# First batch of a relative-attention layer: keys of all chunks projected first, ones written by ScalarE, loads placed singly

## The reference

```python
rk, rv = embK[dist], embV[dist]
logits = einsum('bhqd,bhkd->bhqk', q, k) + einsum('bhqd,qkd->bhqk', q, rk)
w = softmax(logits)
out = einsum('bhqk,bhkd->bhqd', w, v) + einsum('bhqk,qkd->bhqd', w, rv)
out = out.reshape(tokens, 256) @ Wo.T + bo
```

## Time and profile before

| | us |
|---|---|
| median of 3 runs | 2489.82 |
| profiled execution, its time | 2489.01 |
| its span, first to last instruction | 2487.2 |
| TensorE busy in the span | 2360.2 (95%) |
| VectorE busy | 2072.3 (83%) |
| ScalarE busy | 1533.3 (62%) |
| GpSimd busy | 955.0 (38%) |

### The profile page before, as it was taken

One profiled execution on the slowest core, in us unless ns is written; L12 is line 12 of the kernel. 1 busy time (PEld: TensorE's weight loads), 2 busy tenths in 40 slices (PEclk: granted clock), 3 DMA queues, 4 the chain that ended last, 5 costly groups with the idle time before them and its releaser, 6 DMA issues.

```text
span 2487.2 us, 100503 instructions
## 1 busy us (share of the span) xinstructions
PE 2360.2 (95%) x41858; PEld 1743.2 (70%) x41858; DVE 2072.3 (83%) x5306; ACT 1533.3 (62%) x2993; POOL 955.0 (38%) x2219
## 2 busy tenths in 40 slices
PE   4599999999999999999999999999999999999995
PEld 3277777777777777777777777777777777777773
DVE  5588789987898878987899878998789887998886
ACT  2366666666666666666666666666666666666651
POOL 5001634435343444425444263443534344442024
PEclk8699999999999999999999999999999999999998
DMA  4766675567656576565755667466765657656520
GB/s 137 230 194 181 201 206 149 163 176 220 182 155 184 166 209 191 158 182 180 200 171 166 189 194 205 147 169 179 216 187 149 183 174 206 194 144 192 153 57 30
DMA packets 659031, 433.24 MB, mean 174 GB/s; under 512 B 204304, under 2 KB 657680, under 8 KB 658448
## 3 DMA queue, kind: packets, MB, share of 16 engines
q1 hardware_dynamic: 655632, 424.52, 58.7%
q10 hardware_dynamic: 2944, 2.29, 0.3%
HBM read 231.30 MB, written 194.79 MB: 171 GB/s over the span
## 4 chain that ended last, share of the span: by engine, by line
PE 67%; DVE 23%; issue 6%; SPq 2%; ACT 1%; POOL 1%; DMA 1%; DVEq 0%; POOLq 0%; ACTq 0%
PE logitsT L955 16%; PE oacc L979 14%; PE scores L928 10%; DVE junk L1231 7%; PE logitsT L959 7%; DVE maxes L1225 7%; PE misc L883 5%; PE misc L1004 2%; PE misc L991 2%; PE misc L1043 2%; PE misc L900 2%; PE misc L911 2%; DVE stats L1101 2%; PE misc L1015 1%; DVE mv L1104 1%
## 5 line engine op out<-in xcount | busy, mean ns | idle before, releaser
L955 PE MATMUL logitsT<-qs,ks 98*128 98x128 bf16 (+1 forms) x8192 | 878.4, 221 | 7.6 <-ACT wy L1445 3.0
L1231 DVE CUSTOM_DVE_ANT_1 junk<-scores,bands 128x512 bf16<-128x512 f32 x988 | 679.6, 688 | 188.5 <-issue 79.1
L1445 ACT ACTIVATE wy<-logitsT 128x512 f32<-128x512 f32 x1024 | 561.6, 596 | 375.0 <-PE logitsT L955 367.7
L1225 DVE TENSOR_REDUCE maxes<-scores 128x1 f32<-128x512 f32 x1024 | 656.6, 682 | 81.8 <-PE scores L928 79.2
L955 PEld LDWEIGHTS logitsT<-qs,ks 98*128 98x128 bf16 (+1 forms) x8192 | 582.9, 99 | 183.5 <-issue 96.4
L928 PE MATMUL scores<-mks,mqs 48*128 48x256 bf16 (+6 forms) x3712 | 445.0, 289 | 20.5 <-DMA mks<-kd 10.8
L959 PE MATMUL logitsT<-ident,bands 128*128 128x128 f32 x2048 | 410.3, 278 | 0.9 <-issue 0.9
L1445 ACT ACTIVATE wr<-logitsT 128x512 f32<-128x512 f32 x512 | 314.3, 614 | 127.8 <-PE logitsT L955 126.3
L1474 POOL TENSOR_SCALAR rs<-rs 128x1 int32<-128x1 int32 (+1 forms) x217 | 46.4, 214 | 716.5 <-DVE rs L1106 709.5
L959 PEld LDWEIGHTS logitsT<-ident,bands 128*128 128x128 f32 x2048 | 292.7, 143 | 20.4
L1479 POOL TENSOR_SCALAR rs<-rs 128x1 f32<-128x1 f32 x744 | 279.2, 378 | 64.9
(11 more groups left out here) (145 smaller groups left out, 2951.9 us busy)
## 6 DMA issues: line engine op xcount, KB each, us to landing
bs<-praw SPq DMA_DIRECT2D x256, 512.0 KB, 4.5
bands<-bs SPq DMA_DIRECT2D x224, 512.0 KB, 4.5
ks<-kd SPq DMA_DIRECT2D x64, 384.0 KB, 5.0
qs<-qd SPq DMA_DIRECT2D x112, 198.0 KB
bands<-bs SPq DMA_DIRECT2D x128, 128.0 KB, 2.8
mks<-kd SPq DMA_DIRECT2D x128, 96.0 KB, 3.7
qd<-qparts SPq DMA_DIRECT2D x60, 192.0 KB, 3.5
qd<-qparts SPq DMA_DIRECT2D x90, 128.0 KB, 3.1
```

What stands on the lines that cost most here:

```text
L955: mm = e.matmul(lt[:, j * P:(j + 1) * P], kk[0:depth, SLOT[HB * blk + j], kt * P:(kt + 1) * P], qs[i][0:depth, SLOT[HB * blk + j], :], sta ...
L1225: e.tensor_reduce(top, sc[:], AX.X, ALU.max).then_inc(row_maxed, 1)
L1231: e.tensor_tensor_reduce(junk[:], sc[:].rearrange("p (a c) -> p a c", a=2), banded, 1.0, LOWEST, ALU.add, ALU.max, top).then_inc(row_maxed, 1)
L1445: e.activation(dst, src, ACT.Exp).then_inc(exp_ready, 1)
```

## The change

It concerns the first batch and the order of what stands before the body:

- Every stage of every chunk of the first batch has a slot of its own, and so has every load, band product, band write and band read of steps 0 to 3. The order on TensorE becomes: turn chunk 0, its queries and keys, far; turn 1, keys 1; turn 2, keys 2; turn 3, keys 3; queries 1, band products of step 0, queries 2, the values of all four chunks, queries 3, band products. SP's list begins: write queries 0, tables, write far 0 and keys 0, load of the queries of step 0, write keys 1, loads of keys 0, write keys 2, and so on; the loads of `mqs` for step 0 stand behind the band reads of step 0.
- The turned tokens of the first batch go to four buffers in `wm` (`xnT0`), the whole values to two (`qf` and `qf1`, in `wy`), and the two buffers of parts alternate by turn of each kind.
- The ones of `ks` and `mks` are copied by ScalarE from one column (`set_ones`, four stages), not set by GpSimd.
- The root of the variance of chunk 1 is taken on VectorE, as that of chunk 0 was.
- `ternary` moves from slot 17.5 to 70.7, three tables are loaded early, two later.
- Weights wait for the keys of their chunk, and every exp of kind Y for the queries and keys of all four chunks to be in DRAM.
- A table `MOVED` of offsets is added; all are zero.

```diff
-    return k == (0, 0) if stage == "statistics" else last_tile(*k) and k[1] % 2 == 1
+    return k in ((0, 0), (0, 1)) if stage == "statistics" else last_tile(*k) and k[1] % 2 == 1
...
- 'write_reltab': -60,
- 'load_table': (-20.0, 3.085, 5.0, 7.0, 9.0),
- 'ternary': 17.535,
+ 'write_reltab': 7.195,
+ 'load_table': (-87.418, -93.996, -1.974, -89.271, 15.194),
+ 'ternary': 70.73,
...
- 'first_chunk': (-100.964, -90.0, -76.951, -69.582),
- 'first_statistics': (-108.7, -102.706, -101.999, -102.4),
- 'first_normalise': (-102.964, -96.591, -89.5, -79.5),
- 'first_stages': (-0.488, 0.47, 2.57, 4.15, 4.77, 5.8, 6.17, 6.12),
- 'keys_first_stages': (-2.295, 4.08, 6.368, 1.463, 3.0, 8.5, 8.999, 5.33),
- 'first_load_k': (-83.694, -73.717, -63.8, -62.01),
- 'first_load_q': (-89.075, -77.2, -63.496, -53.6),
- 'first_raw': -56.652,
+ 'first_statistics': (-126.982, -110.172, -100.041, -114.031),
+ 'first_normalise': (-122.581, -98.166, -91.967, -92.415),
+ 'first_turn_x': (-127.001, -91.9, -89.91, -87.142),
+ 'first_project_q': (-99.088, -82.669, -75.918, -67.483),
+ 'first_project_k': (-95.791, -89.944, -87.157, -87.02),
+ 'first_project_v': (-71.556, -69.597, -69.117, -67.976),
+ 'first_far': (-92.427, -75.978, -74.577, -60.882),
+ 'first_write_q': (-98.98, -71.174, -66.486, -2.531),
+ 'first_write_far': (-88.947, -70.236, -64.976, 1.597),
+ 'first_write_k': (-88.674, -84.11, -76.658, -76.184),
+ 'set_ones': (-90.174, -100.193, -13.676, -18.47),
+ 'tables': -90.896,
+ 'far_table': -107.135,
+ 'first_load_k': (-83.082, -16.776, -2.916, -66.931),
+ 'first_load_mk': (-83.437, -76.217, -70.748, -70.051),
+ 'first_load_q': (-86.403, -69.735, -50.089, -13.616),
+ 'first_load_mq': (-68.98, -29.789, -69.55, -33.317),
+ 'first_raw': ((-80.243, -77.423), (-66.484, -18.53), (-9.275, -17.406), (-1.629, 0.564)),
+ 'first_band_write': ((-74.618, -69.88), (-62.905, -57.295), (-15.284, -18.422), (-2.366, -1.745)),
+ 'first_band_read': ((-69.993, -69.61), (-36.867, -15.781), (-2.447, -2.048), (2.827, 8.723)),
...
- 'first_load_mk': (-83.13, -73.441, -63.218, -62.73),
...
- 'first_load_mq': (-83.554, -73.717, -61.06, -50.13),
...
-        slots.append((slot, stage, k))
+        slots.append((slot + moved(stage, k), stage, k))
...
-    at(-98.5, "tables")
-    at(-102.1, "far_table")
+    at(x_["tables"], "tables")
+    at(x_["far_table"], "far_table")
+    for i in range(4):
+        at(x_["set_ones"][i], "set_ones", i)
...
-                at(x_["first_statistics"][c], "statistics", b, c)
-                at(x_["first_normalise"][c], "normalise", b, c)
-                for x, stage in zip(x_["keys_first_stages" if keys_first(b, c) else "first_stages"], chunk_stages):
-                    at(x_["first_chunk"][c] + x, stage, b, c)
+                for stage in ("statistics", "normalise") + chunk_stages:
+                    at(x_["first_" + stage][c], stage, b, c)
...
-                x = x_[stage.replace("band_raw", "raw")][blk]
-                at(w0 + x if s else x_["first_raw"] + 12.5 + x, stage, s, blk)
+                name = stage.replace("band_raw", "raw")
+                at(x_["first_" + name][s][blk] if s < QUAD else w0 + x_[name][blk], stage, s, blk)
...
+        qf1 = wy[:, 3, :].rearrange("p (g t) -> p g t", g=G)
+        xnT0 = wm[:].rearrange("p i h q -> p (i h q)")[:, T * H:2 * T * H].rearrange("p (c i t) -> p c i t", c=NCHUNK, i=2)
...
+        first_splits = [x for x in orders["ACT"] if x[0] in ("project_q", "project_k") and x[1][0] == 0]
+        split_turn = {x: i for i, x in enumerate(first_splits)}
+        kind_turn = {x: [y for y in first_splits if y[0] == x[0]].index(x) for x in first_splits}
+        first_split_at = {x: i + 1 for i, x in enumerate(x for x in orders["DVE"] if x in split_turn)}
+        xn_at = {k: i + 1 for i, k in enumerate(k for stage, k in orders["DVE"] if stage == "normalise" and k[0] == 0)}
...
 
-            if b == 0 and c % 2:
+            if b == 0 and kind_turn[stage, (b, c)] % 2:
                 return kparts1 if stage == "project_k" else qparts1
...
+
+        def qf_of(stage, b, c):
+            return qf1 if b == 0 and split_turn[stage, (b, c)] % 2 else qf[:]
+
+        def xnT_of(b, c):
+            return xnT[:] if b else xnT0[:, c]
+
+        def first_of(signal, *stages):
+
+            return max(n(signal, stage, 0, c) for stage in stages for c in range(NCHUNK))
 
...
-            if b or c > 1:
-                pb, pc = ((b, c - 1) if c else (b - 1, NCHUNK - 1)) if b else (b, c - 2)
-                done, count = (k_out, K_OUT) if stage == "project_k" else (q_out, Q_OUT)
+            done, count = (k_out, K_OUT) if stage == "project_k" else (q_out, Q_OUT)
+            if b > 1 or b and c:
+                pb, pc = (b, c - 1) if c else (b - 1, NCHUNK - 1)
...
+            elif b:
+                for pc in range(NCHUNK):
+                    eng.wait_ge(done[0][pc], count)
+            elif kind_turn[stage, (b, c)] > 1:
+                before = kind_turn[stage, (b, c)] - 2
+                for (kind, (_, pc)), turn in kind_turn.items():
+                    if kind == stage and turn == before:
+                        eng.wait_ge(done[0][pc], count)
...
-                    if b or c:
+                    if b > 1 or b and c:
...
-                    e.activation(xnT[:].rearrange("p i t -> p (i t)"), m[:, 0:2 * CT], ACT.Copy).then_inc(xnT_ready, 1)
+                    e.activation(xnT_of(b, c).rearrange("p i t -> p (i t)"), m[:, 0:2 * CT], ACT.Copy).then_inc(xnT_ready, 1)
+                elif stage == "set_ones":
+                    i, = k
+                    act.wait_ge(ones_value_set, 1)
+                    t_, ready, rows, heads = (ks, k_ones_set, ROWS, HG) if i % 2 == 0 else (mks, mk_ones_set, P, PAIRS)
+                    dst = t_[i // 2][:].rearrange("r h s -> r (h s)").bitcast(F32)
+                    e.activation(dst, small[0:rows, 5:6].broadcast_to([rows, heads * S // 2]), ACT.Copy).then_inc(ready[i // 2], 1)
...
-                    if splits(b, c, which) % 2 == 0:
+                    if b == 0:
+                        turn = split_turn[stage, k]
+                        if turn > 1:
+                            act.wait_ge(split_ready[0], first_split_at[first_splits[turn - 2]])
+                    elif splits(b, c, which) % 2 == 0:
...
-                    elif b or c:
+                    else:
...
-                        for dst in (qf,) if b else (qf, parts_buf(stage, b, c)[:, 0]):
+                        for dst in (qf,) if b else (qf_of(stage, b, c), parts_buf(stage, b, c)[:, 0]):
...
+                    elif c == 1:
+                        act.wait_ge(x_turned, first_of("x_turned", "turn_x"))
+                        if s > 1:
+                            act.wait_ge(proj_summed, first_of("proj_summed", "project_q", "project_k"))
+                            act.wait_ge(v_summed, first_of("v_summed", "project_v"))
...
-                        for c_ in (1, 3):
+                        for c_ in range(NCHUNK):
...
-            for t_ in ks:
-                e.memset(t_[:].rearrange("r h s -> r (h s)").bitcast(F32), TWO_ONES).then_inc(k_ones_set, 1)
+            e.memset(small[:, 5:6], TWO_ONES).then_inc(ones_value_set, 1)
...
-            for t_ in mks:
-                e.memset(t_[:].rearrange("r h s -> r (h s)").bitcast(F32), TWO_ONES).then_inc(mk_ones_set, 1)
...
```

More of the change, by code:

```diff
@@ L176 @@
  'end_stages': (0.3, 0.41, 2.11, 2.32, 3.4, 4.16, 4.7, 7.0, 6.85)}
+MOVED = {'row_max': ((0.0, 0.0, 0.0, 0.0, 0.0, 0.0, 0.0, 0.0),
[3 rows of a table added]
+ 'near': ((0.0, 0.0, 0.0, 0.0, 0.0, 0.0, 0.0, 0.0),
[3 rows of a table added]
+ 'rest': ((0.0, 0.0, 0.0, 0.0, 0.0, 0.0, 0.0, 0.0),
[3 rows of a table added]
+ 'weighted': ((0.0, 0.0, 0.0, 0.0), (0.0, 0.0, 0.0, 0.0), (0.0, 0.0, 0.0, 0.0), (0.0, 0.0, 0.0, 0.0)),
+ 'merge': ((0.0, 0.0), (0.0, 0.0), (0.0, 0.0), (0.0, 0.0)),
+ 'band_raw': ((0.0, 0.0), (0.0, 0.0), (0.0, 0.0), (0.0, 0.0)),
+ 'band_write': ((0.0, 0.0), (0.0, 0.0), (0.0, 0.0), (0.0, 0.0)),
+ 'band_read': ((0.0, 0.0), (0.0, 0.0), (0.0, 0.0), (0.0, 0.0)),
+ 'max_reduce': ((0.0,), (0.0,), (0.0,), (0.0,)),
+ 'max_rows': ((0.0,), (0.0,), (0.0,), (0.0,)),
+ 'max_move': ((0.0,), (0.0,), (0.0,), (0.0,)),
+ 'load_q': ((0.0,), (0.0,), (0.0,), (0.0,)),
+ 'load_mq': ((0.0,), (0.0,), (0.0,), (0.0,)),
+ 'relative': ((0.0, 0.0, 0.0, 0.0), (0.0, 0.0, 0.0, 0.0)),
+ 'out_copy': (0.0, 0.0, 0.0, 0.0),
+ 'tail_attT': (0.0, 0.0, 0.0, 0.0),
+ 'tail_wo': (0.0, 0.0, 0.0, 0.0),
+ 'tail_x1': (0.0, 0.0, 0.0, 0.0),
+ 'tail_norm': (0.0, 0.0, 0.0, 0.0),
+ 'tail_normed': (0.0, 0.0, 0.0, 0.0),
+ 'tail_x1T': (0.0, 0.0, 0.0, 0.0),
+ 'tail_ff': (0.0, 0.0, 0.0, 0.0),
+ 'tail_out': (0.0, 0.0, 0.0, 0.0),
+ 'tail_store': (0.0, 0.0, 0.0, 0.0),
+ 'turn_x': (0.0, 0.0, 0.0, 0.0),
+ 'project_q': (0.0, 0.0, 0.0, 0.0),
+ 'far': (0.0, 0.0, 0.0, 0.0),
+ 'project_k': (0.0, 0.0, 0.0, 0.0),
+ 'project_v': (0.0, 0.0, 0.0, 0.0),
+ 'statistics': (0.0, 0.0, 0.0, 0.0),
+ 'normalise': (0.0, 0.0, 0.0, 0.0)}
@@ new lines, in moved @@
```

(39 more changed lines are left out.)

37 lines of the change are left out of this document (19 added, 18 removed), and 9 rows, old and new, of the table MOVED.

## The result

The changed kernel took 2465.03 us (median of four runs, 2461.84 to 2466.99), the kernel before 2489.07 on the same chip (four runs, 2487.59 to 2492.89): ratio 0.990, 95% interval 0.9883 to 0.9917. The forecast was 2470, with 2460 to 2483 as its range. The profiled execution after has a span of 2462.7 us, 24.5 less than the 2487.2 before.

What follows compares the result with a forecast made beforehand. TensorE fills the body; the 108.4 us opening, where everybody waits, is what changes. First weights 108.4 to 87.5, less 21, given back 2: 2489 - 19 = 2470 us, range 2460 to 2483.

Steps and rivals of the forecast that it cites:

- the better rival: Opening: band and scores meet early, clock at its upper level; scores from 60, weights at 80, 2462 us; chance 0.1.
- Ones: Start of opening: moving the fill off GpSimd frees VectorE of 7.2 us of waits, 4.7 kept at the first write.
- The second root on VectorE: Chunk 1's root beside GpSimd's: might wait step by step; by the strictest reading first write some 5 us later.
- no release of VectorE: Rival: VectorE's two steps slow by themselves, or strict port rule; first write at 25.9, all 4.7 later, 2475; chance 0.1.
- Keys first: Opening, keys of chunks 1 to 3 before later queries: chunk 3's keys written by 43.7, landed at 47.
- Loads: SP's list: `mqs` of step 0 out at 64.4, landed at 66.7, last of all, so the scores start there.
- From the scores to the weights: End of opening: step 0's maxima end at 78.5, six of step 1's take 9 more, first weights at 87.5.
- three ends: Before the first weights: VectorE's maxima, the maxima's move on SP and ScalarE's band-copy wait meet at 86 to 88.
- The band of step 2: After the first weights: its band read out at 88.9, landed at 93.6, wanted at about 91.5; 2 us lost.
- Ternary: Body, ternary step moved from slot 17.5 to 70.7: its halt moves along, cost 0.
- rivals of round trips: Opening: loads waiting for just-issued writes keep DMA at 187 GB/s; first weights at 98, 2481 us; chance 0.25.
- a slower kernel: Rival: the DMA rate of 24 to 64 us holds throughout the opening; first weights at 133, 2514 us; chance 0.04.

## Why the prediction was right, and where it was off

The mechanism was the forecast one: an opening shortened while TensorE's body stays. The step off was the sum's first term, first weights at 87.5: measured 84.19, 3.3 less. The second term, 2 us given back after it, was net 0.3 the other way (2378.8 to 2378.5). So 2465.03 lies between the forecast and the better rival (scores from 60, weights at 80: 2462). Of that rival's two grounds the early scores came in part and the clock did not: it was granted at 0.50 from 64 to the weights. Step by step:

- *Ones.* Normalise done by 8.95, first write at 21.2: measured 8.85 and 21.37. ScalarE's copies 3.6 and 1.9: measured 3.61 and 1.90. That the steps of VectorE were slow because of GpSimd's fill was inferred from two ends that coincide; putting the fill back and taking it out alone both show it. Not foreseen: of the 4.35 us that the fill costs at the first write, only 2.5 arrive at the weights. With the fill put back TensorE has none of its later waits for `mqs` of step 0 and step 1 (0.38 and 1.97 in the changed kernel) and for the moved maxima (0.43); they take the rest.
- *The second root on VectorE* was not held: its pairs took 0.46 and 0.34 us beside GpSimd's root of chunk 3, as the ones of chunk 0 did alone (0.45 and 0.34). So the rival "no release of VectorE" falls in both its forms. It was GpSimd that suffered: beside VectorE's split its pairs took 1.43 and 1.30 (0.67 and 0.51 otherwise), and VectorE waited 2.24 us at normalise of chunk 2 for them. The Trainium skill, page "SBUF — State Buffer", section "Who interferes with whom", says that a VectorE instruction with two inputs in SBUF contends with a GpSimd one that reads SBUF; the split has two such operations, so by that rule the trace agrees. A cast of the split (0.43 us) runs beside the pairs too, and no run takes the two apart.
- *Keys first.* Last write of keys out by 43.7: measured 42.43. Undoing it cost 4.05 us at the weights.
- *Loads.* `mqs` of step 0 out at 64.4: measured 58.69. This is the mis-sized term, and it grew link by link: the last keys were out 1.3 us earlier than forecast, the first band write 2.2 (at 45.2, its issue done at 43.04), the queries of chunk 1 3.7 (written from 48.0, measured 44.29), the second band write 5.1 (out at 57.1, measured 52.02), this load 5.7. The reason given, that the scores start when this load lands, is half of it: TensorE did wait for the load, 0.38 us in the changed kernel and 1.83 in its second run, but with the load 25 us earlier the scores start no earlier, since TensorE's own list gets there at about that point. Two ends met, and I had seen one.
- *From the scores to the weights.* Forecast 66.7 to 87.5, 20.8 us; measured 62.81 to 84.19, 21.4. (In the working 66.7 and 12.1 make 78.8, not 78.5; by its own numbers the sum comes to 87.8.) The maxima were the forecast chain: step 0's took from 62.81 to 74.84, 12.0 us. Counted at nothing was TensorE's wait of 1.97 us for `mqs` of step 1. Of the three ends that I let meet at 86 to 88, the band copy's wait did end there (83.82, behind a band write), but the last to come was one whose landing I hadn't counted: the maxima's move, issued from 78.15 to 79.61 (forecast done at 82), releasing the weights 6.04 after its start. It was last by 0.43 us. In all 14 traces, the kernel before among them (102.24 to 108.41), the first weights start 5.50 to 6.55 us after that issue, but only three of them show TensorE waiting for it (0.43, 0.17 and 0.34). In the others the weights follow the scores of step 1 with no wait, and the distance tells of a common start, not of a cause. In eight it is 5.50 to 5.59: the chain of step 1's maxima on TensorE and VectorE starts at the same point as the move, since the transpose of step 0's maxima stands on TensorE's list behind the first scores of step 1. In the three with the old order it is 6.17, and TensorE comes there from a wait for ScalarE's band copy (3.60 us in the kernel before, until 103.03).
- *The band of step 2.* Forecast out at 88.9 and 2 us late: it was issued at 83.95, and the first steps after the start ran faster than before. By the moves of the maxima the lead was 24.1 us at the first (78.15 against 102.24), 25.5 at 120.0 (145.5), 26.3 at 221.3 (247.6) and 24.0 at 284.6 (308.6).
- *Ternary* was costed at nothing, "its halt moves along". It moved from 146.09 to 232.85 and doubled. TensorE's rows, before and after:

```profile
146.09 0.38 PE L864 MATMUL misc<-small,ybuf 128*128 128x1 f32 x2 [0.83 <-DVE small L1167]
```
```profile
232.85 0.38 PE L958 MATMUL misc<-small,ybuf 128*128 128x1 f32 x2 [1.67 <-DVE small L1270]
```

  The lead follows these two halts: it rises by 0.7 us across the first (25.5 to 26.2) and falls by 2.4 across the second (26.3 to 23.8). Net 1.7 us are given back there, 0.84 of it the longer halt; the rest I have not traced to a row.
- *Rate.* 227 GB/s was needed from the first write on, and 165 was the point from which it would go slower. Measured from the first write to the weights, columns as in the earlier trace rows:

```profile
21.37:84.19 62.82, 44.83 (x193) 24.90 (x194) 41.83 (x99) 27.35 (x49) 10.94 (x23) 0.69 0.82 243
```

  The whole opening ran at 222 (187 before). The rivals of round trips and of a slower kernel fall with that.

What stays open: of the 16.6 to 21.7 us of order and loads, some 4 are shown for keys first (chunks 1 and 2). The second buffer's share is too small to be told; the loads' share can't be had alone, since moving them in the old order only moved the halt. Four buffers for turned tokens were not tried by themselves.

## What to carry to other kernels

An opening that waits on a chain is costed by its links: follow what releases the end, row by row, and ask which wait ends last. A row at a constant distance ahead of the end (here the move of the maxima, 5.5 to 6.5 us ahead of the weights) is a place to look and not yet a cause: three traces of 14 show a wait for it. Where two ends meet within a microsecond or two, moving one earlier gives little: of five kernels that each relieved something in the opening, none was faster than the changed kernel by what can be measured. And one profile is one draw: the same program started its weights at 80.2 and at 83.6.

## What was not expected of the hardware

*The clock after a short halt.* In the changed kernel and ten variants of it TensorE halts for 1.67 us at the ternary step, and what follows differs from run to run. These are the stretches of 4 us around the halt and 6 us behind it, columns as in the earlier trace rows: the changed kernel, then the one with `mqs` of step 2 late.

```profile
230.85:234.85 4.00, 2.33 (x39) 1.80 (x42) 3.46 (x9) 2.42 (x6) 3.70 (x5) 1.00 0.60 177
234.85:240.85 6.00, 6.00 (x60) 4.91 (x53) 5.69 (x16) 1.79 (x4) 0.23 (x1) 1.00 0.33 92
```
```profile
228.71:232.71 4.00, 2.33 (x19) 1.91 (x18) 3.25 (x9) 1.63 (x5) 3.69 (x5) 0.75 0.60 177
232.71:238.71 6.00, 6.00 (x52) 4.20 (x51) 4.90 (x13) 1.01 (x2) 0.37 (x1) 0.60 0.03 8
```

The same halt leaves the granted clock at its upper level in the one and, in the other, partly at the 1.2 GHz level; over the 10 us that is 4 x 0.25 + 6 x 0.40 = 3.4 us of full clock at most. Measured from the move of the maxima ahead of the halt to the one behind it, the stretch took 23.07 us in the one (221.35 to 244.42) and 25.75 in the other (219.22 to 244.97). By these moves that kernel's lead over the changed one went from 2.1 us (168.8 against 170.9) to 0.7 behind it (285.3 against 284.6) across this place: most of what it gave back was lost here. Five of the eleven traces show such a dip (0.60 to 0.83 over the 6 us behind the halt; that stretch takes 24.2 to 25.8 us), six show none (23.0 to 23.4 us), and both kinds occur with the same halt. In the 6 us behind it DMA is at a share of 0.03 to 0.09 in the traces with the dip and 0.30 to 0.33 in those without; around the halt, where the clock has begun to fall, the shares are alike (0.59 to 0.61), so the emptier DMA looks like a result. What decides it no run here tells.

*The price of an issue.* Four loads of `mqs` took SP 3.93, 4.15 and 5.42 us at the same place of its list, the first and the last in one and the same program: 1.5 of the 3.4 us between its two profiles.
